# Context attention: exchange and half of the placing DMAs issued by ScalarE, the next context load in front of the placing, the input scaled ahead of the rotation

## The reference

```python
x = x + _L1_xattn_ref(_layernorm(x, axis=-1), ctx_1024, ctx_1024, L1_xattn_Wq, L1_xattn_Wk, L1_xattn_Wv, L1_xattn_Wo, L1_xattn_bo)

def _L1_xattn_ref(query, key, value, Wq, Wk, Wv, Wo, bo):   # 16 heads of 16
    q = split_heads(query @ Wq.T)
    k = split_heads(key @ Wk.T)
    v = split_heads(value @ Wv.T)
    q = _apply_rope(q)      # first half x1, second half x2 of a head:
    k = _apply_rope(k)      # [x1 cos - x2 sin, x1 sin + x2 cos]
    logits = jnp.einsum('bhqd,bhkd->bhqk', q, k) * scale
    attn = jax.nn.softmax(logits, axis=-1)
    out = jnp.einsum('bhqk,bhkd->bhqd', attn, v)
    out = out.transpose(0, 2, 1, 3).reshape(b, t, d)
    return out @ Wo.T + bo
```

## Time and profile before

| | us |
|---|---|
| median of 3 runs | 4451.44 |
| lowest, highest | 4448.23, 4452.7 |
| profiled execution | 4454.12 |
| its span on the core | 4452.1 |
| TensorE busy in the span | 4044.9 (91%) |
| VectorE, ScalarE, GpSimd busy | 2702.6, 1893.0, 266.9 |
| first and last placing DMA issued at | 2101.9, 2887.5 |

### The profile page before, as it was taken

How to read it: one execution, slowest core, us unless ns; L and a number is a source line. 1 busy time by engine, 2 the same in 40 slices (tenths; PEclk the granted TensorE clock), 3 DMA queues, 4 the chain that set the end, 5 groups by cost and what they waited for, 6 DMA issues and landing times. The chain is left out here.

```text
span 4452.1 us, 88171 instructions
## 1 busy us (share of the span) xinstructions
PE 4044.9 (91%) x30632; PEld 2836.1 (64%) x30632; DVE 2702.6 (61%) x5798; ACT 1893.0 (43%) x5106; POOL 266.9 (6%) x389
## 2 busy tenths in 40 slices
PE   7999899999999798886688788879999989999999
PEld 6887455555555566774455555558888756666666
DVE  5777466666665466775455555547777645555555
ACT  4777455555555222442234333336666611111111
POOL 0000111111110000110000000000000000000000
PEclk9999899999999899998899999989999989999999
DMA  6000000000000000000222222224444420000000
GB/s 140 0 0 0 19 13 15 14 13 15 14 13 8 1 0 1 0 0 16 59 56 59 55 58 56 52 59 130 127 126 126 126 76 5 5 5 5 5 5 9
DMA packets 178390, 165.50 MB, mean 37 GB/s; under 512 B 98681, under 2 KB 159106, under 8 KB 178050
## 3 DMA queue, kind: packets, MB, share of 16 engines
q1 hardware_dynamic: 177296, 160.58, 14.4%
q10 hardware_dynamic: 882, 1.92, 0.1%
HBM read 75.49 MB, written 55.05 MB: 29 GB/s over the span
## 5 line engine op out<-in xcount | busy, mean ns | idle before, releaser
L2291 DVE SCALAR_TENSOR_TENSOR g_residual<-m_out,m_gate,g_residual 112x256 f32 (+1 forms) x1280 | 549.6, 479 | 420.8 <-PE m_out L2140 416.2
L2140 PE MATMUL m_out<-e_down,m_hidden 128*112 128x256 f32 x2560 | 603.3, 379 | 0.0
L2140 PEld LDWEIGHTS m_out<-e_down,m_hidden 128*112 128x112 f32 x2560 | 452.5, 177 | 192.5 <-issue 112.7
L2129 PE MATMUL m_hidden_bank<-m_xT,e_up 128*128 128x448 f32 x1280 | 538.7, 546 | 2.7 <-issue 2.7
L2191 ACT ACTIVATE m_hidden<-m_hidden_bank 128x448 f32<-128x448 f32 x256 | 139.0, 543 | 647.0 <-PE m_hidden_bank L2129 647.0
L1705 DVE TENSOR_REDUCE x_top<-x_scores 112x4 f32<-112x1500 f32 x128 | 219.9, 1718 | 263.7 <-PE x_scores L1567 261.6
L2129 PEld LDWEIGHTS m_hidden_bank<-m_xT,e_up 128*128 128x128 f32 x1280 | 240.6, 192 | 149.8 <-issue 133.6
L1112 ACT ACTIVATE x_probs<-x_held,x_minus_top 112x488 f32<-112x488 f32 x256 | 177.4, 694 | 264.3 <-DVE x_minus_top L1168 264.3
L1819 PE MATMUL r_ring<-w_pT,r_q 128*112 128x224 f32 x1024 | 240.7, 370 | 17.8 <-ACT r_by_position L821 13.4
L1023 PE MATMUL x_ring<-w_xkv,x_kv 128*122 128x512 f32 x512 | 233.4, 599 | 15.7 <-ACT x_k L821 15.0
L1016 PE MATMUL x_ring<-x_kv,w_xkv 128*128 128x488 f32 x512 | 240.9, 594 | 0.0
(11 more groups left out here) (286 smaller groups left out, 7510.9 us busy)
## 6 DMA issues: line engine op xcount, KB each, us to landing
by_position<-r_by_position SPq DMA_DIRECT2D x128, 392.0 KB, 3.1
r_bias<-by_position SPq DMA_DIRECT2D x128, 196.0 KB, 3.2
x_ctx<-in_ctx SPq DMA_DIRECT2D x64, 375.0 KB
x_kq_swapped<-x_kq_raw SPq DMA_DIRECT2D x64, 243.5 KB, 4.3
x_slots<-x_kq SPq DMA_DIRECT2D x512, 30.4 KB
e_up<-in_L_ffn_keys SPq DMA_DIRECT2D x16, 256.0 KB, 6.5
e_down<-in_L_ffn_values SPq DMA_DIRECT2D x8, 512.0 KB, 6.7
g_residual<-in_x SPq DMA_DIRECT2D x4, 896.0 KB, 12.9
```

Of the source, the lines that this page charges most:

```text
L2129: ins = nc.tensor.matmul(hidden_bank[e % 2][:, 0:Q * T], M["up"][:, f, e, :], xT[par][:, f, :], start=(f == 0), stop=(f == DC - 1))
L2140: ins = nc.tensor.matmul(out_bank[2 * (e % 2) + i // 2][0:T, (i % 2) * D:(i % 2 + 1) * D], hidden[e % 2][:, i * T:(i + 1) * T], M["down"][ ...
L2291: nc.vector.scalar_tensor_tensor(row, out_bank[2 * (e % 2) + i // 2][0:T, (i % 2) * D:(i % 2 + 1) * D], gate[par][0:T, i, e:e + 1], row, A ...
```

## The change

Four edits, all in ContextAttention.

1. The exchange is no longer issued by SyncE behind a signal of GpSimd. ScalarE issues it in step `k1`, behind its copy of k1, after waiting for its own copies of q, k0 and k1. The semaphore `kq_ready` and GpSimd's part of `k1` go.
2. The placing is split by halves of the head. SyncE issues the eight DMAs of the first half as before. The eight of the second half are issued by ScalarE in a new step `place` of age 2, that is at the start of the frame behind the one of the rotation, between headsB and back0.
3. SyncE loads the context of batch e + 1 in frame e, once ctx0 of batch e is copied out, in front of the placing of batch e - 1. It loads one batch sooner.
4. `scale` stands in front of `ctx0` and `rope` in the list, no longer behind `project`.

```diff
-        self.plan = Flow(4, [("g0", 3), ("headsB", 5), ("back0", 5), ("tr0", 4), ("q", 1), ("k0", 1), ("g1", 3), ("k1", 1),
+        self.plan = Flow(4, [("g0", 3), ("headsB", 5), ("place", 2), ("back0", 5), ("tr0", 4), ("q", 1), ("k0", 1), ("g1", 3), ("k1", 1),
                              ("back1", 5), ("stats", 0), ("tr1", 4), ("v0", 2), ("v1", 2), ("g2", 3), ("v2", 2), ("onT", 5),
-                             ("ctx0", 0), ("rope", 1), ("tr2", 4), ("project", 5), ("scale", 0), ("ctx1", 0), ("g3", 3), ("xT", 0),
+                             ("scale", 0), ("ctx0", 0), ("rope", 1), ("tr2", 4), ("project", 5), ("ctx1", 0), ("g3", 3), ("xT", 0),
                              ("headsA", 4), ("put", 3)],
...
-        def swap(b):
-
-            sp.wait_ge(self.kq_ready, b + 1)
-            for i in range(2):
-                sp.dma_start(self.kq_swapped[64 * i:64 * (i + 1), :, :],
-                             self.kq_raw[64 * (1 - i):64 * (2 - i), :, :]).then_inc(self.swapped, 16)
-
         def place(b, par):
 
             sp.wait_ge(self.place_ready, b + 1)
-            for half in range(2):
-                for r in range(2):
-                    for a in range(HS):
-                        src = 64 * half + 8 * (HS * r + a)
-                        dst = SLOT * a + 8 * half
-                        sp.dma_start(self.slots[par][dst:dst + 8, r::2, :],
-                                     self.kq[src:src + 8, :, :]).then_inc(self.slotted, 16)
+            self.place_half(sp, par, 0)
 
         def body(e, par):
             N = self.plan.turns
-            if not isinstance(e, int) or 0 < e < NB:
-                self.ready(sp, "ctx0", e - 1)
-                load(e, par)
-            if not isinstance(e, int) or 0 <= e - 1 < NB:
-                swap(e - 1)
+            if not isinstance(e, int) or e + 1 < NB:
+                self.ready(sp, "ctx0", e)
+                load(e + 1, (par + 1) % N)
             if not isinstance(e, int) or 0 <= e - 1 < NB:
                 place(e - 1, (par - 1) % N)
         load(0, 0)
-        frames(sp, NB, body, ahead=self.plan.ahead, behind=self.plan.behind, turns=self.plan.turns)
+        frames(sp, NB - 1, body, ahead=self.plan.ahead - 1, behind=self.plan.behind + 1, turns=self.plan.turns)
+
+    def place_half(self, eng, par, half):
+
+        for r in range(2):
+            for a in range(HS):
+                src = 64 * half + 8 * (HS * r + a)
+                dst = SLOT * a + 8 * half
+                eng.dma_start(self.slots[par][dst:dst + 8, r::2, :], self.kq[src:src + 8, :, :]).then_inc(self.slotted, 16)
...
-        elif name == "k1":
-            self.ready_all(pool, ("q", "k0", "k1"), b)
-            pool.sem_inc(self.kq_ready, 1)
...
+            if name == "k1":
+
+                self.ready_all(act, ("q", "k0", "k1"), b)
+                for i in range(2):
+                    act.dma_start(self.kq_swapped[64 * i:64 * (i + 1), :, :],
+                                  self.kq_raw[64 * (1 - i):64 * (2 - i), :, :]).then_inc(self.swapped, 16)
...
+        elif name == "place":
+            act.wait_ge(self.place_ready, b + 1)
+            self.place_half(act, par, 1)
```

More of the change, by code:

```diff
@@ L1464, in __init__ @@
         super().__init__(nc, G, W)
-        self.plan = Flow(4, [("g0", 3), ("headsB", 5), ("back0", 5), ("tr0", 4), ("q", 1), ("k0", 1), ("g1", 3), ("k1", 1),
+        self.plan = Flow(4, [("g0", 3), ("headsB", 5), ("place", 2), ("back0", 5), ("tr0", 4), ("q", 1), ("k0", 1), ("g1", 3), ("k1", 1),
                              ("back1", 5), ("stats", 0), ("tr1", 4), ("v0", 2), ("v1", 2), ("g2", 3), ("v2", 2), ("onT", 5),
-                             ("ctx0", 0), ("rope", 1), ("tr2", 4), ("project", 5), ("scale", 0), ("ctx1", 0), ("g3", 3), ("xT", 0),
+                             ("scale", 0), ("ctx0", 0), ("rope", 1), ("tr2", 4), ("project", 5), ("ctx1", 0), ("g3", 3), ("xT", 0),
                              ("headsA", 4), ("put", 3)],
-                         bankless=("tr0", "tr1", "tr2", "g0", "g1", "g2", "g3", "rope", "stats", "scale"), ahead=8, behind=5, turns=3)
+                         bankless=("tr0", "tr1", "tr2", "g0", "g1", "g2", "g3", "rope", "place", "stats", "scale"), ahead=8, behind=5, turns=3)
     def allocate(self, sb, sem):
@@ L1488, in allocate @@
         self.flipped_ready, self.exped = sem("flipped_ready"), sem("exped")
-        self.kq_ready, self.place_ready = sem("kq_ready"), sem("place_ready")
+        self.place_ready = sem("place_ready")
     def sync(self, sp):
```

## The result

The changed kernel takes **4545.01 us**, median of 4 runs (4539.99 to 4552.67); before, in the same session, 4450.69 us (4448.23 to 4452.7). The ratio is 1.0214, with a 95% interval of 1.0196 to 1.0231: 94 us slower. The prediction said 4547.

A forecast was written before the change was run, and what follows sets the result against it. TensorE was fullest, its idle time filled by a ring through SyncE. A frame of 21.46 + 4.0 + 0.15 + 1.5 + 0.4 = 27.5 us gave +106.5 + 4 - 15 = +96 us, so 4547 us; range 4450 to 4575.

The forecast's parts named there:

- The eight issues on ScalarE: ScalarE's queue, between headsB's copy and tr0's exponential: 5.9 us of placing issues make the exponential 4.6 us late, g1 4.0.
- The price of an issue: Placing DMA on ScalarE: 686 ns each, as on SyncE; bounds 465 ns and 0.
- The clock: TensorE behind the new 4.0 us idle time ahead of g1: lower clock costs 1.5 us a frame, bounds 0 and 2.0.
- The exchange on ScalarE: Behind ScalarE's copy for k1: two DMA issues of 1.18 us fit a 1.15 us gap but for about 0.15 us.
- The rotation against g3: VectorE's queue: g3's reduction waits behind rotation and scaling, 0.4 us a frame, taken between 0 and 0.8.
- Frame and jumps: Layer 1 context attention: frames of 27.5 us, 29 of them 797.5; seven loop jumps at 4.8 us make 831, before 724.5.
- The first frames: Start of the stage, no exponential to delay: two frames of about 17 us in place of 25.0 give back 15 us.
- The frame behind: One frame behind the 29 also has a placing on ScalarE: +4 us.
- A: Rival: ScalarE's issues cost only 465 ns, g1 2.3 us late, clock falls half the time; 4470 us, chance 0.11.
- B: Rival: issues hidden, exponential delayed under 0.4 us, and the ring through SyncE was the bound; 4368 us, chance 0.12.
- C: Rival: SyncE's and ScalarE's placing halves overlap by 1 us, paid twice; frame 0.7 us longer, 4567 us, chance 0.04.
- The statement on the ring: SyncE's queue: placing, context load, exchange, waits for it and VectorE's rotation, placing again after 24.7 us; this fills TensorE's idle time.

The follow-up runs named there:

- the third part alone: The kernel before with only the next context load moved in front of the placing on SyncE: 4383.67 us, ratio 0.9849.
- the other two parts, alone: The kernel before with only the input scaled ahead of the rotation, 4450.6 us; and with only the exchange issued by ScalarE, 4442.23 us.

## Why the prediction was right, and where its sizes were off

The total was 2 us from the measured median, and the mechanism is the one it told. What was off are the sizes of some terms. Its steps:

- **The eight issues on ScalarE** (predicted: exponential 4.6 us late, 0.4 absorbed, g1 4.0 late). Right. They took 5.90 us, g1 was 3.9 late, and the two kernels with four and two issues show the cover that it used: 1.8 us from the start of the copy to the exponential, and 0.4 us behind k0. What made this term good was the place at which the idle time was read: 1.34 us between the copy and the exponential, not ScalarE's 63% of the stage. The Trainium skill (Perfetto Trace Analysis, section DMA Instruction — HWDGE (DVE, Sync)) has the sequencer held until the descriptors are made; the trace of after agrees, with 5.73 us of "issue" in front of the exponential.
- **The price of an issue** (686 ns, bound 465). Right: 697 ns. The form set it and not the engine.
- **The clock** (1.5 us, bounds 0 and 2.0). The mechanism was right, the size too small: 2.1 us in a typical frame by the kernel with the tripled k0, just outside the bound, and 1.7 us as a mean over the 29. The value was taken from behind a jump, with some slack for the larger k1; k1 alone grew from 1.53 to 2.87 us, g1 by 0.71.
- **The exchange on ScalarE** (0.15 us). Right: 0.1 to 0.2. g1 to g2 is 5.94 to 6.01 us in the kernels with it at full clock, 5.83 in those without. It landed in 3.4 us, not in 4.3, because the load is no longer close to it, and not because the queue is another: alone, on ScalarE and with the load close, it took 4.1 in the median. Its gain alone was 8 us, all in the first frames.
- **The rotation against g3** (0.4 us). It did not come: g2 to g3 is 5.7 to 5.8 us in the changed kernel as in the undisturbed frames of the one before, g3 to g0 3.8. The value was taken between bounds of 0 and 0.8 and the lower one was true.
- **Frame and jumps.** Predicted 27.5 and 4.8 us, measured 27.66 and 5.3 (g3 to g0 7.1 to 7.6 in place of 3.8, g0 to g1 11.4 to 12.3 in place of 10.1). The clock too small and the rotation too large cancel within the frame. 29 frames: predicted 831, measured 837.1 (29 of 27.66 and the jumps would be 839; the frames with a shorter drop of the clock are under 27.66).
- **The first frames** (-15 us) gave -20.1: the first placing begins 3.4 us sooner, which I did not count, and the next two stand 15.3 and 17.8 us apart, in place of 25.0 and 24.1; I had 17.
- **The frame behind** (+4) took +5.0.

So the sum was +96 by the predicted terms and +98.7 by the two spans, with misses of +6, +1 and -5 that nearly cancel. Against the profiled execution of after, 4552.67 us, the working gave 4550. That the median came within 2 us has luck in it: the runs of after alone spread over 12.7 us.

**The rivals.** A fell with the 697 ns. B's price, 4368 us, was for the ring gone and the issues hidden. The kernels where that is so take 4380 to 4384: it was 12 to 16 us too low, mostly since the 29 frames take 665 to 672 us there and not 656. In the kernel with the load alone (664.8) a frame is 21.54 us and not 21.46, the first of the 29 takes 24.0, and a jump costs 5.0 us by the kernel with six frames a turn and up to 5.5 by the rows, not 4.8; the exchange on ScalarE adds 0.1 to 0.2 us a frame where it is. Its condition (the exponential late by under 0.4 us) holds with two issues and fails with four. C had its condition and not its price. SyncE's eight issues begin 2.7 us ahead of g0 (2562.49 and 2565.16 above), not 3 us into the frame as the prediction had it, and in 21 of the 29 placings behind the first three they still run when ScalarE's begin, by 0.7 to 1.8 us, the overlap of 1 us that C counts with. Yet ScalarE's eight take 5.9 to 6.2 us with it and 5.9 to 6.3 without. The Trainium skill (Perfetto Trace Analysis, section DMA Optimizations) says that balancing issues over the engines that have a queue may help where descriptor generation is the bottleneck. The runs here narrow it: SyncE's 12 us of issues lay in the ring, yet what helped was the order in that queue (4384 us with all 16 on SyncE); balancing eight of them cost 161 us against that kernel and two nothing, by what stood behind the issues.

**The statement on the ring** was right, and stronger than it was put: the third part alone opens it and gives all of the gain, and the other two parts, alone, only move the wait to the next members (but for the 8 us that the exchange gains in the first frames).

## What to carry to other kernels

A DMA issue takes its engine's in-order queue for its whole length, so measure the gap at that very place in the queue (1.3 us here, room for two issues of 0.74) and ask who waits for the instruction behind it; the engine's share of idle time says nothing on it. In a ring of waits, look for the step that doesn't need to be in it (a load queued behind a transfer it doesn't depend on) and move that one; shortening the others moves the wait. And price an idle time of TensorE with what the clock takes behind it: 3.8 us of idling cost another 1.7 here on average, 2.1 in most frames.

## What the runs showed of the hardware

- TensorE, idle for 3.8 us in each frame, was granted the low level (0.50) behind it, and the 4.5 us of work that followed took 2.1 us longer in most frames. Seven frames have 7.1 to 7.6 us from g1 to g2, between the 6.0 without a drop and the 8.1 with one. With 1.3 to 1.4 us of idling at the same place there was no drop in the frames shown. But 3.8 us are not needed for one: in the kernel before, the low level stands behind the 1.99 us for which TensorE waits for xn in the frame of the earlier trace rows. The view by stages, kernel before:

```profile
2526.53:2529.95 3.42, 3.36 (x52) 2.78 (x53) 2.07 (x3) 0.58 (x2) 0.00 (x0) 0.50 0.25 35
```

- ScalarE and SyncE issue the same DMA at nearly the same price (697 and 686 ns). Where both issue at once, ScalarE's median rises to 726 ns and SyncE's stays.
- The exchange, two DMAs of 64 partitions, lands in 4.0 to 7.9 us where the context load is issued within 4 us of it, from the same queue (before) or another (the exchange on ScalarE alone), and in 3.0 to 3.6 where the load is further off. With the load moved, the median is 3.4 to 3.6.
- A jump of the loop costs TensorE some 3.5 us of idling (7.1 to 7.9 us from g3 to g0 in place of 3.8), whether three or six frames stand in a turn, and 1.1 to 2.6 us behind it by the clock. Four jumps fewer gave 20 us.
